# Output projection and layer norm of the first attention, placed at the end of the heads' program

## The reference

```python
out = av.transpose(0, 2, 1, 3).reshape(b, s, e) @ Wo + bo      # block 1: full attention, 16 heads of 8
x = layernorm(embedding + out)                                 # the part that this change is about
# block 2: two layers of windowed attention (8 heads of 64) and a gated feed-forward
# block 3: attention with a Taylor softmax; block 4: a feed-forward with integer weights
```

## Time and profile before

| | us |
|---|---|
| median of three runs (1818.91 to 1823.56) | 1821.44 |
| the profiled execution | 1818.25 |
| its span in the trace | 1816.5 |

### The profile page before, as it was taken

How to read it: one execution, slowest core, us unless ns; L and a number is a source line. 1 busy time by engine, 2 the same in 40 slices (tenths; PEclk the granted TensorE clock), 3 DMA queues, 4 the chain that set the end, 5 groups by cost and what they waited for, 6 DMA issues and landing times. The chain is left out here.

```text
span 1816.5 us, 41434 instructions
## 1 busy us (share of the span) xinstructions
PE 1612.7 (89%) x14986; PEld 815.6 (45%) x14986; DVE 1420.4 (78%) x2971; ACT 1260.4 (69%) x2564; POOL 791.2 (44%) x609
## 2 busy tenths in 40 slices
PE   6599999999999999659999888889998879799887
PEld 4122332323222322336666565556666656444454
DVE  6799999999999998268888886478888869433355
ACT  5178888888888888519999883169998854455421
POOL 4201122112211233358888862278887735644311
PEclk9589999999999999859999999989999999798999
DMA  5203110000000000120020002201020012000001
GB/s 166 63 21 132 35 38 19 22 23 26 23 19 19 19 20 2 42 63 19 24 51 24 23 18 71 61 10 27 25 58 24 21 44 71 1 1 1 1 12 36
DMA packets 114224, 62.49 MB, mean 34 GB/s; under 512 B 48562, under 2 KB 108908, under 8 KB 113772
## 3 DMA queue, kind: packets, MB, share of 16 engines
q1 hardware_dynamic: 112636, 58.79, 11.4%
q10 hardware_dynamic: 1392, 1.12, 0.2%
HBM read 42.82 MB, written 16.79 MB: 33 GB/s over the span
## 5 line engine op out<-in xcount | busy, mean ns | idle before, releaser
L947 DVE TENSOR_REDUCE hd_top<-hd_pX 128x1 f32<-128x512 f32 x1024 | 624.1, 682 | 32.6 <-PE hd_pX L791 32.6
L917 ACT ACTIVATE hd_E<-hd_pS 128x1024 f32<-128x1024 f32 x512 | 524.7, 1025 | 82.4 <-PE hd_pS L807 60.1
L791 PE MATMUL hd_pX<-l_K,l_Q 48*128 48x512 bf16 x1024 | 342.8, 396 | 26.1 <-DMA l_Q<-q_parts 21.5
L824 PE MATMUL hd_pO<-hd_E,l_V 128*32 128x256 f32 x4096 | 327.6, 392 | 18.1 <-ACT hd_O L892 17.9
L807 PE MATMUL hd_pS<-l_Q,l_K 50*128 50x512 bf16 x1024 | 310.8, 384 | 2.7 <-DMA l_Q<-hd_negp 1.6
L739 POOL TENSOR_TENSOR hd_inv<-hd_OS,hd_minus 128x16 f32<-128x16 f32 x32 | 92.8, 2900 | 454.1 <-ACT hd_OS L905 441.5
L1402 ACT ACTIVATE w_pS<-w_pS,w_nb 128x128 f32<-128x128 f32 x512 | 177.9, 358 | 39.4 <-DVE w_nb L1497 39.3
L1437 POOL TENSOR_TENSOR w_C<-w_C,w_N 128x1024 f32<-128x1024 f32 x64 | 151.2, 2362 | 109.7 <-DVE w_N L1471 109.5
L1448 POOL TENSOR_TENSOR w_inv<-w_ss,w_mhalf 128x16 f32<-128x16 f32 x64 | 186.4, 2913 | 0.0
L824 PEld LDWEIGHTS hd_pO<-hd_E,l_V 128*32 128x32 f32 x4096 | 81.8, 108 | 172.0 <-issue 125.4
L807 PEld LDWEIGHTS hd_pS<-l_Q,l_K 50*128 50x128 bf16 x1024 | 59.0, 94 | 197.6 <-issue 184.3
(11 more groups left out here) (278 smaller groups left out, 2923.9 us busy)
## 6 DMA issues: line engine op xcount, KB each, us to landing
l_Q<-q_parts SPq DMA_DIRECT2D x192, 32.0 KB
l_K<-k_parts SPq DMA_DIRECT2D x168, 32.0 KB
m<-early_rows SPq DMA_DIRECT2D x64, 64.0 KB, 1.7
f_H<-m SPq DMA_DIRECT2D x32, 128.0 KB, 2.7
f_X<-m SPq DMA_DIRECT2D x16, 256.0 KB, 3.1
q_parts<-pj_ptq SPq DMA_DIRECT2D x8, 384.0 KB, 2.5
k_parts<-pj_ptk SPq DMA_DIRECT2D x8, 384.0 KB
pj_X<-in_L_attn_embedding_dram SPq DMA_DIRECT2D x8, 256.0 KB, 3.2
```

The lines of the kernel that those rows point to most:

```text
L791: nc.tensor.matmul(px[:, :], Q[m.j][rows, m.z, b, t * P:(t + 1) * P], K[m.j][rows, b, k * 512:(k + 1) * 512], start=True, stop=True).then_ ...
L824: last = nc.tensor.matmul(pO[VW * b:VW * b + VW, cols], V[n.j][:, b * NT + g, :], E[g % SLOTS][:, b, cols], start=(g == 0 and half == 0), ...
L917: nc.scalar.activation(E[g % SLOTS][:, 2 * k:2 * k + 2, :], pS[k][:, :, :], ACT.Exp).then_inc(exped[k], 1)
L947: nc.vector.tensor_reduce(top2[m.z][:, ROW_ORDER[q], k:k + 1], pX[slot][:, :], AX.X, ALU.max).then_inc(topped, 1)
```

## The change

`phase_project_norm` is gone; its work is in a class `ProjectTail` whose methods run at the end of the heads' program.

- Chunks are taken in the order 0, 2, 4, 6, 1, 3, 5, 7 (`ORDER`): the first four belong to z = 0, whose rows in `attn` are complete before unit 31 is. PE transposes the first two before the last products of unit 31, straight from `attn`.
- `norm` of unit 31 is done by DVE from PSUM, with a reciprocal. `take_out` of unit 31 is gone.
- SP issues all 8 loads of the embedding rows behind the last store of negated maxima, into `token_rows`; POOL adds the bias to all 8 behind its last unit.
- The sum is made in place in `token_rows`, and normalised in place by ACT: four activations with scale rstd and bias -mean x rstd, which DVE makes (`shift`) for chunk i-1 behind the statistics of chunk i.
- PE multiplies chunk i and transposes chunk i+2 behind it; there are two transposed chunks and four product banks. ACT copies transposed chunk i and then normalises chunk i-2.
- The heads' semaphores are cleared behind the first window layer and no longer before block 2; the semaphores and the barriers of the third program are gone.

```diff
-def phase_l0_heads(nc, kept, a, q_parts, k_parts, v_all, attn, operands):
+class ProjectTail:
+    ORDER = list(range(0, T // CH, 2)) + list(range(1, T // CH, 2))
+    HALF = len(ORDER) // 2
+    def __init__(self, nc, s, kept, attn, x_in_d, x_out_d, landing, following, pX, pS):
+        self.nc, self.kept, self.attn, self.landing, self.following = nc, kept, attn, landing, following
+        rows = lambda x: x.rearrange("b (j t p) d -> b j p t d", t=CT, p=P)
+        self.x_rows, self.out_rows = rows(x_in_d), rows(x_out_d)
+        self.chunks = kept.token_rows[:, :, :].rearrange("p (c t) d -> p c t d", t=CT)
+        self.room, self.AT = kept.mixer_in, kept.mixer_in["HT"]
+        self.pX, self.pY = pX, [pS[y // 2][:, y % 2, :] for y in range(4)]
+        self.x_in = s.sems("x_in", len(self.ORDER))
+        (self.half_set, self.turned, self.at_ready, self.made, self.biased, self.added, self.var_ready, self.rstd_ready,
+         self.shift_ready, self.normed, self.stats_step, self.stats_passed) = (
+            s.sem(n) for n in "half_set turned at_ready made biased added var_ready rstd_ready shift_ready z_normed stats_step stats_passed".split())
+    def banks(self, slot):
+        return [self.pX[(slot + 1) % 3], self.pX[(slot + 2) % 3]]
+    def load(self, sp):
+        for i, c in enumerate(self.ORDER):
+            sp.dma_start(self.chunks[:, c], self.x_rows[c // 2, c % 2]).then_inc(self.x_in[i], 16)
+    def store(self, sp):
+        for i, c in enumerate(self.ORDER):
+            if i == 2:
+                sp.wait_ge(self.landing.sems[0], 16)
+                self.following.load(sp)
+            sp.wait_ge(self.normed, i + 1)
+            sp.dma_start(self.out_rows[c // 2, c % 2], self.chunks[:, c]).then_inc(self.landing.sems[i % 2], 16)
+    def gpsimd(self, pool):
+        r = self.room
+        nc = self.nc
+        nc.gpsimd.memset(r["mhalf"][:, :], -0.5).then_inc(self.half_set, 1)
+        bias = self.kept.bo0[:, :].rearrange("p (t d) -> p t d", t=1).broadcast_to([P, CT, D])
+        for i, c in enumerate(self.ORDER):
+            pool.wait_ge(self.x_in[i], 16)
+            nc.gpsimd.tensor_tensor(self.chunks[:, c], self.chunks[:, c], bias, ALU.add).then_inc(self.biased, 1)
+        pool.wait_ge(self.half_set, 1)
+        for i in range(len(self.ORDER)):
+            j = i % 2
+            pool.wait_ge(self.var_ready, i + 1)
+            if i > 1:
+                pool.wait_ge(self.normed, i - 1)
+            nc.gpsimd.tensor_tensor(r["rstd"][:, 0, j], r["veps"][:, 0, j], r["mhalf"][:, :], ALU.pow).then_inc(self.rstd_ready, 1)
+    def turn(self, pe, i, pT):
+        c = self.ORDER[i]
+        if i > 1:
+            pe.wait_ge(self.at_ready, i - 1)
+        for t in range(CT):
+            last = self.nc.tensor.transpose(pT[i % 2][:, t * P:(t + 1) * P], self.attn[:, c * CT + t, :], self.kept.ident[:, :])
+        last.then_inc(self.turned, 1)
+    def project(self, pe, i):
+        pe.wait_ge(self.at_ready, i + 1)
+        if i > 3:
+            pe.wait_ge(self.added, i - 3)
+        for t in range(CT):
+            last = self.nc.tensor.matmul(self.pY[i % 4][:, t * P:(t + 1) * P], self.AT[:, i % 2, t * P:(t + 1) * P], self.kept.wo0[:, :],
+                                         start=True, stop=True)
+        last.then_inc(self.made, 1)
+    def take(self, act, i, pT):
+        act.wait_ge(self.turned, i + 1)
+        if i > 1:
+            act.wait_ge(self.made, i - 1)
+        self.nc.scalar.copy(self.AT[:, i % 2, :], pT[i % 2][:, :]).then_inc(self.at_ready, 1)
+    def normalise(self, act, i):
+        r, j, c = self.room, i % 2, self.ORDER[i]
+        act.wait_ge(self.shift_ready, i + 1)
+        for t in range(CT):
+            last = self.nc.scalar.activation(self.chunks[:, c, t, :], self.chunks[:, c, t, :], ACT.Identity,
+                                             bias=r["shift"][:, 0, j, t:t + 1], scale=r["rstd"][:, 0, j, t:t + 1])
+        last.then_inc(self.normed, 1)
+    def add(self, dve, i):
+        r, j, x = self.room, i % 2, self.chunks[:, self.ORDER[i]]
+        dve.wait_ge(self.made, i + 1)
+        dve.wait_ge(self.biased, i + 1)
+        self.nc.vector.tensor_tensor(x, self.pY[i % 4].rearrange("p (t d) -> p t d", t=CT), x, ALU.add).then_inc(self.added, 1)
+        dve.wait_ge(self.added, i + 1)
+        if i > 1:
+            dve.wait_ge(self.rstd_ready, i - 1)
+            dve.wait_ge(self.shift_ready, i - 1)
+        st = Step(dve, self.stats_step, 2, i, self.stats_passed)
+        norm_stats(self.nc, dve, st, r["stats"], r["mv"][:, 0, j], r["veps"][:, 0, j], x).then_inc(self.var_ready, 1)
+    def shift(self, dve, i):
+        r, j = self.room, i % 2
+        dve.wait_ge(self.rstd_ready, i + 1)
+        if i > 1:
+            dve.wait_ge(self.normed, i - 1)
+        self.nc.vector.scalar_tensor_tensor(r["shift"][:, 0, j], r["mv"][:, 0, j, :, 0], -1.0, r["rstd"][:, 0, j], ALU.mult, ALU.mult)\
+            .then_inc(self.shift_ready, 1)
+    def tensor_first(self, pe, pT):
+        for i in range(2):
+            self.turn(pe, i, pT)
+    def tensor_rest(self, pe, pT, last_ready, pH):
+        n = len(self.ORDER)
+        for i in range(n):
+            self.project(pe, i)
+            if i + 2 == self.HALF:
+                pe.wait_ge(last_ready, 1)
+            if i + 2 < n:
+                self.turn(pe, i + 2, pT)
+        self.following.turn(pe, pH)
+    def scalar_rest(self, act, pT, pH):
+        n = len(self.ORDER)
+        self.take(act, 1, pT)
+        for i in range(2, n):
+            self.take(act, i, pT)
+            self.normalise(act, i - 2)
+        self.normalise(act, n - 2)
+        self.following.take(act, pH)
+        self.normalise(act, n - 1)
+    def vector(self, dve):
+        for i in range(len(self.ORDER)):
+            self.add(dve, i)
+            if i > 0:
+                self.shift(dve, i - 1)
+        self.shift(dve, len(self.ORDER) - 1)
+def phase_l0_heads(nc, s, kept, a, q_parts, k_parts, v_all, attn, operands, x_out_d, landing, following):
...
     FOLD_AT = (2 * ROWS - AHEAD) // 2 - 1
     TURN_AT = FOLD_AT + 1
     CLOSE_AT = 2
-    with ExitStack() as ctx:
-        s = Scope(nc, ctx, "hd")
+    with s.ctx:
         ident = kept.ident
         Q, K, V = operands
         E = [s.sb(f"E{j}", [P, B, HQ]) for j in range(SLOTS)]
...
         O = s.sb("O", [P, HQ])
         OS = s.sb("OS", [P, HQ])
         inv = s.sb("inv", [P, QT, B])
+        last_inv = s.sb("last_inv", [P, QT, B])
         ones = s.sb("ones", [P, 1])
         minus = s.sb("minus", [P, 1])
         pS = [s.ps(f"pS{j}", [P, 2, HQ]) for j in range(2)]
...
         o_taken = s.sem("o_taken")
         inverted = s.sem("inverted")
         normed = s.sem("normed")
+        last_inverted, last_normed = s.sem("last_inverted"), s.sem("last_normed")
+        tail = ProjectTail(nc, s, kept, attn, a["L0_attn_embedding"], x_out_d, landing, following, pX, pS)
         LOADS = 16 * 2 * GROUPS * len(PART_PAIRS)
         NEGS = 16 * MAX_ROWS * GROUPS
...
                         head(R * i + j, j)
                 for h in range(H - R, H):
                     head(h, h % R)
+                for j in range(R):
+                    sp.wait_ge(v_ready[j], H // R)
+                tail.load(sp)
+                tail.store(sp)
             @block.gpsimd
             def _(pool):
...
                 part_neg(Unit(0))
                 kept.finish_mixer(pool)
                 units(unit)
-                norm(Unit(UNITS - 1))
+                tail.gpsimd(pool)
             @block.tensor
             def _(pe):
...
                 units(unit)
                 last = Unit(UNITS - 1)
+                pT = tail.banks(banks.at % RING)
+                pe.wait_ge(topped, TOPS * UNITS)
+                pe.wait_ge(o_taken, UNITS - 1)
+                pe.wait_ge(normed, UNITS - 1)
                 products(last, NT - 2, 1)
+                tail.tensor_first(pe, pT)
                 for half in range(2):
                     products(last, NT - 1, half)
                 close(last, TOPS * UNITS)
+                for k in range(2):
+                    pe.wait_ge(exped[k], NT * UNITS)
+                tail.tensor_rest(pe, pT, last_normed, pT[0])
             @block.scalar
             def _(act):
...
                 take_neg(Unit(0))
                 pass_tops(2 * (AHEAD - ROWS))
                 units(unit)
+                pT = tail.banks(banks.at % RING)
+                tail.take(act, 0, pT)
                 take_sums(Unit(UNITS - 1))
-                take_out(Unit(UNITS - 1))
+                tail.scalar_rest(act, pT, pT[0])
             @block.vector
             def _(dve):
...
                             banks.take("out")
                 units(unit)
-def phase_project_norm(nc, tag, attn, x_in_d, x_out_d, kept, landing, following):
...
+                last = Unit(UNITS - 1)
+                dve.wait_ge(o_turned, UNITS)
```

(16 more changed lines are left out.)

126 lines of the change are left out of this document (removed).

## The result

The changed kernel takes 1807.14 us (median of 20 runs), the kernel before on the same chips 1819.83 (20 runs); the ratio is 0.9909, with a 95% interval from 0.9890 to 0.9928. The ratio is lower than that of the two medians, 0.9930: six of the 20 runs before took 1828 to 1837 us, and only two of the 20 after more than 1820. The forecast was 1807.0 us and faster by more than 0.3%. In two later series, in which the unedited changed kernel ran again, the ratio was 0.9917 (0.9900 to 0.9933) and 0.9934 (0.9911 to 0.9958).

The account below looks back on a forecast made before the run. No engine was full: DVE, partly held by POOL, and the fixed order of a turn bound the changed stage. Gains 7.81 + 7.81 - 0.36 - 0.87 = 14.4 us, against the 1821.44 median, gave 1807.0 us; range 1803.0 to 1812.5.

Parts of the forecast that it names:

- rival B: Tail: PE's clock stays at 1.2 GHz from product 3 on; gain 12.6 us, 1808.9 us; chance 0.18.
- Loads and bias: Under unit 31: row loads and POOL's bias additions are done before the first sum needs them; cost nothing.
- First sum: From `close` to DVE's first sum: 1.15 us, with the transposes' 0.84 us 1.99 against 9.80; 7.81 us gained.
- The pace: First to eighth sum: ACT's queue paces, 4.68 us plus product per two chunks; 20.62 us against 28.43, 7.81 gained.
- A: Tail: PE's clock stays at 2.4 GHz throughout; gain 15.3 us, 1806.1 us; chance 0.15.
- The end: From the eighth sum to block 2's first product: 6.73 us against 6.37, 0.36 lost.
- The heads' clearing: Semaphore clearing that comes back behind the first window layer: 0.87 us lost.
- The first layer of block 2: First window layer: changes by no more than 1 us beside the clearing; PE starts at half clock in both kernels.
- C: Tail: POOL's power holds DVE's shift, 1.06 us more per link of the two-chunk chain; 1810.3 to 1813.1 us; chance 0.12.
- D: Start of tail: rows or bias late, sums wait or shifts are held, 1.05 us each; 1811.4 us; chance 0.05.
- E: Heads' loop loses pace: 0.45 us per unit eats the gain, 0.62 us makes 1827 us; chance 0.03.
- F: Tail: straight-line code stalls in fetching, old pace of 4.06 us per chunk; gain 6.6 us, 1814.8 us; chance 0.07.

Follow-up runs that it names:

- late_rows: Changed kernel, but SP issues the eight row loads only once unit 31's sums are copied; `close` to block 2 took 36.52 us.
- after: The changed kernel, unedited, first series and its trace, against the kernel before the change; 1807.14 us, ratio 0.9909.
- transposes_behind: Changed kernel, but the first two chunks are transposed behind unit 31's last products and sums, not ahead; single run 1823.14 us.
- after_5: The changed kernel, unedited, in five rounds against the kernel before the change; 1808.9 us, ratio 0.9934.
- extra_copy: Changed kernel, with ACT copying each transposed chunk from the fourth on once more into an unread tile; sum 0 to 7 took 23.87 us.
- clear_at_once: Changed kernel, but the heads' semaphores are cleared right behind the heads' program, ahead of block 2; `close` to block 2 took 30.44 us.
- before: The kernel without the change, and its trace; 1819.83 us, median of 20 runs.
- takes_first: Changed kernel, but ACT copies chunks 1 to 3 before normalising any, then normalises chunk i-4 before copying chunk i; 1800.43 us.
- takes_first_5: The kernel of takes_first, no further edit, in five rounds beside the unedited changed kernel; 1803.13 us, ratio 0.9891.
- again: The changed kernel once more, unedited, for a second trace; 1806.59 us, ratio 0.9917.
- dve_normalises: Changed kernel, but four DVE instructions normalise in place of the shift and ACT's activations; single run 1810.07 us.

## Why the prediction was right, step by step

The time, its range and the chain that paces the tail came out as forecast. Two of its own signs did not: product 7 took 2.07 us, which it lists as the sign of rival B, and the first window layer changed by 1.6 us, more than the 1 us at which it calls itself wrong. Both stand below.

**Loads and bias at nothing: right.** POOL's norm of unit 30 ended at 740.13 (estimate 739), the additions at 750.03 (749), and the first sum came 1.8 us later. late_rows shows what lies under that cover: 8.4 us, more than half of what the tail gains.

**Transposes ahead of the last products: right.** Forecast 0.84 us later for `close`; 0.76 in after and 0.77 from transposes_behind.

**First sum: right, slightly pessimistic.** 0.92 to 0.93 us behind `close` in every trace with the change but two (late_rows and transposes_behind, where the edit moved it), against 1.15. The product of chunk 0 begins while PE's transposes end and takes 1.06 us, not 1.13.

**The pace: mechanism and size right, the clock right by luck.** The link of 4.68 us and the product gives 5.84 and 6.75 us for the two product times; measured are 5.84, 5.80 and 6.71. The forecast had one of the three links at half clock, the first; in after it was the last, in after_5 two of the three were, in extra_copy all, and sum 0 to 7 took 20.59, 20.95 and 21.52 us in three traces of one kernel (21.79 in clear_at_once, whose tail is the same), against 20.62. The reason given for product 3, an idle stretch of 3.2 us before it, did not hold in after: PE stood idle 3.83 us there, and the product took 1.16. Which product meets a low clock couldn't be read from the trace of before; only the span from A (19.70) to B (22.46) could, and all four lie in it.

**The end: right.** 6.61 us against 6.73.

**The stage as a whole.** 28.13 us in the profile, 28.1 to 29.1 over three, against 28.5. The kernel before had 44.60.

**The heads' clearing: mis-sized.** 0.87 us was the time between two rows of the clearing; the whole is 1.1.

**The first layer of block 2: wrong.** I had block 2 unchanged within 1 us, because its PE starts at half clock in both kernels. It does (the first product took 3.75 us in both), but the clock did not take the same course from there. From its first product to the last residual addition it took 303.05 us before (to 1096.63) and 304.65 after (to 1083.69). The first tile is 2.0 us longer. Busy time by stretches, counted from the start of block 2 the same 28 us on, in before, in takes_first, and in takes_first_5:

```profile
821.55:825.55 4.00, 3.93 (x48) 2.10 (x46) 3.19 (x7) 3.78 (x9) 3.92 (x2) 1.00 0.00 0
```
```profile
801.15:805.15 4.00, 4.00 (x49) 2.29 (x47) 3.19 (x7) 3.77 (x12) 3.92 (x3) 1.00 0.02 4
```
```profile
803.72:807.72 4.00, 4.00 (x28) 1.69 (x30) 2.06 (x7) 2.76 (x11) 3.92 (x3) 0.57 0.01 4
```

In the first two PE had the full clock and the tile took 36.3 and 36.7 us; in the third the clock was 0.57, as in after (807.01 to 811.01, above), and the tile took 38.3. In these four microseconds the clock was 0.57 to 0.60 in after, again, after_5, takes_first_5, extra_copy, transposes_behind and clear_at_once, with a first tile of 38.2 to 38.5 us and a whole window layer of 304.6 to 305.0; it was 1.00 in before, takes_first and dve_normalises, with 36.3 to 36.7 us and 303.0 to 303.2. late_rows lies between in the clock (0.64) and near the short ones in time (36.98 and 303.29). takes_first and takes_first_5 are one kernel and have one of each, so it is no fixed cost of the change. That the length goes with the clock there is what the traces show, and late_rows says that it doesn't follow this stretch alone; whether the tail's new timing brings it about more often (in all three traces of the changed kernel, not in the one of before) stays open, since I have only one trace of before.

**The sum.** Forecast 14.4 us. In the two profiles block 2 starts 14.54 us earlier; without the 1.17 us by which the heads of this execution were later, it is 15.71, against the forecast of 15.26. The window layer takes back 1.6, the second clearing 1.2 as the distance between the two, and the later stages, whose code is the same, 1.0 (single stages between 1.0 shorter and 1.4 longer): 14.54 - 1.6 - 1.2 - 1.0 = 10.7. The medians differ by 12.7, 14.6 and 11.4 us in the three series, the ratios stand for 16.6, 15.1 and 12.0. The 1807.0 was right to 0.1 us, and that is partly luck: it started from a median of three runs, 1821.44, where twenty give 1819.83, and this 1.6 us made up for a gain that came out 1.7 us smaller (12.7 for 14.4).

**The rivals.** A and B were both partly true, as single links of the chain. C did not come about: the shift took 0.15 to 0.16 us each time. The reason is not the one I gave. DVE issues it right behind the variance, and POOL's power starts only when it has ended (the shift 758.67 + 0.15, the next power in POOL's queue from 758.84 on), so the two did not meet. What did run beside the power was not held: the sum at 756.44, with one input in PSUM, took 0.68 us, and in dve_normalises four instructions took 1.11. In late_rows the two did meet, and the shift, with both its tensor inputs in SBUF, took 0.16 us inside a power of 1.01. The Trainium skill, in "GPSIMD Engine Reference", Specifications, has GpSimd contend with VectorE instructions that have two SBUF inputs. The addition of the earlier trace rows agrees with that, this power does not, so the mechanism of C is refuted too, by one meeting. D came true only when forced, and by another way than I had it. E is refuted: from the first copy of a unit's sums to the end of `close` it was 629.51 us before and 629.65, 630.20 and 631.23 in three traces of the changed kernel, 0.76 of it the transposes, where E wanted 14 us or more; and PE executed the same 584 instructions in 60 us in the middle of the heads. F is refuted: sums 2.9 us apart and not 4.06.

## What to carry to other kernels

When work of one kind moves to an idle engine, look at what stands behind it in that engine's queue: here the copy that feeds PE stood behind the moved normalising, and the move gave 0.9 us at most until the copies were put one chunk ahead. A chain that is written as a link (so much, and the product) can be checked by adding a known copy to it, which gave the link to 0.05 us, and by taking the order away, which left the pace of the next engine, 2.34 us for an estimate of 2.35. Work under cover is worth pricing as well: the early loads and additions cost nothing that the traces show and save 8.4 us. And where one engine holds another, that holding wants a price of its own: here it was 5.7 us.

## What the runs showed of the hardware

- POOL's additions of 128 x 512 hold DVE: eight normalising instructions took 4.27 us beside two of them and 2.36 without, and a shift 1.22 in place of 0.17. POOL's power of 128 x 4 did not hold a shift (0.16 us in late_rows), four normalising instructions (1.11) or a sum (0.68).
- Clearing a program's semaphores with its two barriers costs 1.1 us at each of two places in the program, with no cover from the work around it.
- Four activations of 128 x 128 with scale and bias from SBUF take 1.65 us on ACT and leave its queue free after 1.55; four DVE instructions for the same take 1.11.
- The granted clock of PE in a stage with gaps differs between executions of one kernel: product 3 took 1.16, 1.51 and 2.08 us in three traces. With transposes that nobody reads (PE busy 19.66 us of 26.30) the clock stayed at 2.4 GHz through the tail of one trace; that was worth 0.9 to 1.8 us in the tail and nothing that the medians show.
- A stage of 175 us, with the same instructions, took 189.3 us in one trace at a mean clock of 0.80 in place of 0.88: a single run can be off by more than the whole effect, and only the stage tells.
